# Normalised rows scattered into expert order: a routing pass whose pair table and row gathers give way to one read per slot

## What is computed

```
x = x + relu(adj_norm @ h @ W_neigh.T + b_neigh + h @ W_self.T + b_self)     # h = layernorm(x), adj is 2048 x 2048
z = layernorm(x)
top 2 of 8 experts for each row by softmax(z @ Wg + bg), weights normalised to sum to 1
x = x + sum over the two experts e of weight_e * (relu(z @ W1[e] + b1[e]) @ W2[e] + b2[e])   # 256 -> 1024 -> 256
```

## Time and profile before

| what | us |
|---|---|
| median of 3 runs (lowest, highest) | 459.83 (457.51, 461.18) |
| span of the profiled execution | 457.5 |
| time of the profiled execution | 457.51 |
| TensorE busy | 386.6 |
| VectorE, ScalarE, GpSimd busy | 331.8, 260.0, 198.4 |

### The profile page before, as it was taken

How to read it: one execution, slowest core, us unless ns; L and a number is a source line. 1 busy time by engine, 2 the same in 40 slices (tenths; PEclk the granted TensorE clock), 3 DMA queues, 4 the chain that set the end, 5 groups by cost and what they waited for, 6 DMA issues and landing times.

```text
span 457.5 us, 10329 instructions
## 1 busy us (share of the span) xinstructions
PE 386.6 (84%) x3029; PEld 373.1 (82%) x3029; DVE 331.8 (73%) x762; ACT 260.0 (57%) x507; POOL 198.4 (43%) x213
## 2 busy tenths in 40 slices
PE   0699899979989920899699989999799998899990
PEld 0477899979989910899699979998799998899990
DVE  5677688867868655388568886887768888688880
ACT  1244533424243150498478874887878887488870
POOL 3000004434543464035445653664645664365663
PEclk9999999999999965699799998999999999899996
DMA  8900445785776111847656776467676677557671
GB/s 250 392 13 0 183 145 203 158 189 154 209 168 183 47 25 25 333 143 248 181 186 224 222 240 174 114 218 230 228 223 224 209 206 242 152 147 225 209 219 14
DMA packets 34526, 81.85 MB, mean 179 GB/s; under 512 B 14797, under 2 KB 28493, under 8 KB 29648
## 3 DMA queue, kind: packets, MB, share of 16 engines
q1 hardware_dynamic: 25616, 73.21, 47.9%
q0 software_dynamic: 8896, 8.48, 10.7%
HBM read 74.51 MB, written 9.77 MB: 184 GB/s over the span
## 4 chain that ended last, share of the span: by engine, by line
PE 68%; DMA 12%; issue 8%; DVE 5%; ACT 2%; SPq 1%; POOLq 1%; POOL 1%; DVEq 0%; ACTq 0%
PE bank L823 28%; PE bank L966 8%; PE bank L967 7%; PE bank L968 7%; PE bank L857 5%; PE bank L859 5%; PE bank L858 5%; DMA adj_raw<-adj_t 4%; PE bank L935 2%; DMA zg<-z_rows,slot_pair 2%; DMA slot_pair<-pairs 2%; DMA y_c<-ws_t 2%; DMA pairs<-pair,slot_i 1%; DVE split L756 1%; PE bank L876 1%
## 5 line engine op out<-in xcount | busy, mean ns | idle before, releaser
L823 PE MATMUL bank<-zt,split 128*128 128x256 f32 x960 | 119.2, 284 | 1.4 <-DVE zt L761 1.4
L823 PEld LDWEIGHTS bank<-zt,split 128*128 128x128 f32 x960 | 117.2, 191 | 1.8 <-DVE zt L761 1.8
L469 ACT ACTIVATE split<-w_raw 128x1024 fp32r<-128x1024 f32 x84 | 87.0, 1072 | 37.5 <-PE bank L968 21.1
L756 DVE TENSOR_TENSOR split<-w_raw,split 128x1024 fp32r<-128x1024 f32 x84 | 100.6, 1220 | 6.5 <-ACT split L469 6.1
L384 POOL DMA_INDIRECT out<-y_c,kept x40 | 72.6, 1814 | 63.8 <-ACT y_c L513 55.8
L966 PE MATMUL bank<-split,h_hi 128*128 128x256 f32 x320 | 94.5, 295 | 0.0
L967 PE MATMUL bank<-split,h_hi 128*128 128x256 f32 x320 | 91.4, 286 | 0.0
L968 PE MATMUL bank<-split,h_lo 128*128 128x256 f32 x320 | 91.3, 285 | 0.0
L367 POOL DMA_INDIRECT zg<-z_rows,slot_pair x44 | 60.8, 1383 | 69.0 <-issue 45.3
L491 ACT ACTIVATE h_raw<-bank,b_sb 128x256 f32<-128x256 f32 x160 | 72.1, 482 | 18.6 <-PE bank L823 18.2
L782 DVE TENSOR_TENSOR h_lo<-h_raw,h_hi 128x512 fp32r<-128x512 f32 x80 | 55.3, 692 | 32.8 <-ACT h_hi L494 31.5
(11 more groups left out here) (122 smaller groups left out, 454.9 us busy)
## 6 DMA issues: line engine op xcount, KB each, us to landing
w_raw<-w SPq DMA_DIRECT2D x22, 2048.0 KB, 8.1
adj_raw<-adj_t SPq DMA_DIRECT2D x16, 1024.0 KB, 6.7
b_sb<-b SPq DMA_DIRECT2D x21, 128.0 KB, 5.1
x_sb<-x SPq DMA_DIRECT2D x4, 512.0 KB, 5.3
out<-x SPq DMA_DIRECT2D x16, 128.0 KB, 3.9
z_rows<-z SPq DMA_DIRECT2D x16, 128.0 KB, 3.9
zg<-z_rows,slot_pair POOLq DMA_INDIRECT x44, 3.5
out<-y_c,kept POOLq DMA_INDIRECT x40, 5.4
```

The costliest lines, as they stand in the source:

```text
L469: act.activation(w_split(b, 0)[:, cols], w_raw[:, b, cols], ACT.Copy).then_inc(w_hi_ready, 1)
L756: dve.tensor_tensor(w_split(b, 1)[:, cols], w_raw[:, b, cols], w_split(b, 0)[:, cols], ALU.subtract).then_inc(w_lo_ready, 1)
L823: last = pe.matmul(o, w, m, start=(n == 0), stop=(n == len(terms) - 1), skip_group_check=True)
```

## The change

The normalised row gets a tail of four words (its row number, the logit difference `DROP`, its first expert `FIRST`) in a ring of four buffers `zr`, and POOL's two indirect DMAs of a tile write the whole 1040-byte row into expert order in a DRAM tensor `rows`, where expert e owns CAP = 2304 rows. `z_rows`, `pairs`, its fill at the start and all `gather` calls are gone. After the last tile, SP writes 256 zero rows behind each expert's last row. A slot is one read of 256 rows. The row numbers for `out` are made by POOL from the tail and a table `past` that puts rows behind an expert's end out of bounds. The table is made on all 128 partitions.

```
 def store(i, b):
     sp.wait_ge(z_ready, i + 1)
     sp.dma_start(out[bass.ds(i * P, P), :], x1[:, b, :]).then_inc(x1_out[b], 16)
-    sp.dma_start(z_rows[bass.ds(i * P, P), :], z[:, b, :]).then_inc(z_out[b], 16)
...
+def load_rows(b, at):
+    sp.dma_start(zg[:, b, :, :], rows[bass.ds(at, SLOT), :].rearrange("(j p) w -> p j w", p=P)).then_inc(row_in[b], 16)
+def fill_after(e, done):
+    at = sp.value_load(fill_at[0:1, e:e + 1], min_val=0, max_val=E * CAP - SLOT)
+    sp.dma_start(rows[bass.ds(at, SLOT), :].rearrange("(j p) w -> p j w", p=P),
+                 zeros[:, None, :].to_broadcast([P, 2, RW])).then_inc(done, 16)
 def ahead(s, b):
     hold(w_lo_ready, 4 * s + 4)
-    if isinstance(s, int) and s == 0:
-        gathered(1)
     load_weights(b, expert(s + 2))
     hold(zt_ps, s + 1)
-    hold(idx_kept, s + 1)
-    hold(ex_ready, s + 1)
-    load_pairs(b, first_row(s + 2))
+    hold(kept_ready, s + 1)
+    hold(coef_step, 3 * s + 3)
+    load_rows(b, first_row(s + 2))
     if not isinstance(s, int) or s >= 1:
         hold(y_biased, s)
     e = expert(s + 1)
     ...  (b1_sb and b2_sb of slot s + 1, unchanged)
...
+sp.wait_ge(fill_ready, 1)
+fill_after(0, first_fill)
+for r in range(RING):
+    for c in range(TOPK):
+        sp.wait_ge(row_out[r][c], 16 * T // RING)
+sp.wait_ge(first_fill, 16)
+load_rows(0, 0)
+for e in range(1, E):
+    fill_after(e, fill_out)
 last = last_of(sp)
-gathered(0)
+sp.wait_ge(fill_out, 16 * (E - 1))
+load_rows(1, first_row(1))
 load_weights(1, expert(1))
```

GpSimd:

```
     for c in range(TOPK):
-        pool.indirect_dma_start(pairs, Rows(slot_i[:, b, c:c + 1], 0), pair[:, b, c, :],
-                                None).then_inc(pair_out[b][c], 16)
+        pool.indirect_dma_start(rows, Rows(slot_i[:, r, c:c + 1], 0), zr[:, r, :],
+                                None).then_inc(row_out[r][c], 16)
...
-def add(s, b):
-    for j in range(2):
-        pool.wait_ge(y_added[j], 16 * s)
-    settle(pool, "pool")
-    keep(1 - b)
-    pool.wait_ge(idx_kept, s + 1)
+def add(s, b, k):
+    pool.wait_ge(row_in[b], 16 * k + 16)
+    pool.tensor_tensor(kept[:, b, None, :], zg[:, b, None, :, TOKEN].bitcast(I32), past[:, bass.ds(s, 1), :],
+                       ALU.add).then_inc(kept_ready, 1)
+    for j in range(2):
+        pool.wait_ge(y_added[j], 16 * s)
+    pool.wait_ge(kept_ready, s + 1)
     pool.wait_ge(y_ready, 2 * s + 2)
     ...  (the two indirect DMAs with addition, unchanged)
 with pool.Fori(0, TURNS) as k:
     with pool.If(k < last + 1):
         for b in range(2):
-            gather(2 * k + b + 2, b, k + 1)
-            add(2 * k + b, b)
+            add(2 * k + b, b, k)
```

More of the change, by code:

```diff
@@ L43, in gnn_moe_kernel @@
     NS = 2 * TURNS + 2
[L44 to L48, removed]
+    RING = 4
+    RW = D + 4
+    TOKEN, DROP, FIRST = D, D + 1, D + 2
+    assert T % RING == 0 and T >= 3 * RING and DC == 2 and FC % 2 == 0 and WCH == F
+    CAP = N + SLOT
+    rows = nc.dram_tensor("rows", (E * CAP, RW), F32, kind="Internal").ap()
     with ExitStack() as ctx:
@@ L95, in gnn_moe_kernel @@
         warm = sb("warm", [P, 2])
[L96 to L110, removed]
+        slot_i = sb("slot_i", [P, RING, TOPK], I32)
+        thr = sb("thr", [P, 8])
+        tri = sb("tri", [P, E, E])
+        iota_s = sb("iota_s", [P, NS])
+        tb8 = sb("tb8", [P, 2, E, E])
+        cnt = sb("cnt", [P, 3, E])
+        ends = sb("ends", [P, 2, E])
+        ge = sb("ge", [P, 3, NS, E])
+        tab_f = sb("tab_f", [P, 6, NS])
+        past = sb("past", [P, NS, 2], I32)
+        zeros = sb("zeros", [P, RW])
+        fill_at = sb("fill_at", [1, E], I32)
+        past_f = sb("past_f", [P, NS, 2])
+        tab = sb("tab", [P, 2, NS], I32)
+        turn_slot = sb("turn_slot", [P, TURNS])
+        used = sb("used", [P, TURNS])
+        last_f = sb("last_f", [P, 1])
+        last_turn = sb("last_turn", [P, 1], I32)
         w_raw = sb("w_raw", [P, 2, WW])
@@ L298, in _ @@
                 hold(w_in[1], 16 * last + 32)
+                hold(row_in[1], 16 * last + 32)
                 for j in range(2):
-                    hold(z_got[1][j], 16 * last + 32)
                     sp.wait_ge(x1_out[j], 16 * T // 2)
@@ L386, in add @@
                                                 compute_op=ALU.add).then_inc(y_added[j], 16)
[L388 to L391, removed]
                 last = last_of(pool)
+                pool.wait_ge(past_ready, 1)
                 with pool.Fori(0, TURNS) as k:
@@ L655, in after, with placing @@
                             settle(dve, "dve")
+                    def placing(step):
+                        place(i - 3, (r + 1) % RING, k4 if r == 3 else k4 - 1, step)
                     dve.wait_ge(acc_done, i + 1)
@@ L659, in turn @@
                     if placed:
-                        place(i - 3, 1 - b, k + b - 2, 0)
+                        placing(0)
                     after(1)
@@ L668, in turn @@
                     if placed:
-                        place(i - 3, 1 - b, k + b - 2, 1)
+                        placing(1)
                     if choose:
@@ L718, in _ @@
                     for step in range(2):
-                        place(i, i % 2, i // 2, step)
+                        place(i, i % RING, i // RING, step)
                 tn = [0]
@@ L767, in slot @@
                         dve.wait_ge(y_ready, 2 * s - 2)
[L768 removed]
+                    dve.scalar_tensor_tensor(out=num[:], in0=zg[:, b, :, FIRST], scalar=tab_f[:, 0, bass.ds(s, 1)], in1=ex[:],
+                                             op0=ALU.is_equal, op1=ALU.max)
+                    dve.tensor_scalar(den[:], ex[:], 1.0, None, ALU.add).then_inc(coef_step, 1)
                     dve.wait_ge(coef_step, 3 * s + 1)
@@ L890, in ranks, with tile @@
                               skip_group_check=True).then_inc(rank_ps, 1)
-                def tile(i, b, back=3):
+                def tile(i, r, back=3):
+                    b = r % 2
                     pe.wait_ge(adj_lo, 2 * i + 1)
@@ L910, in _ @@
                 pe.wait_ge(g_done, T)
-                for i in range(4):
-                    tile(i, i % 2, back=i)
-                with pe.Fori(2, T // 2) as k:
-                    for b in range(2):
-                        tile(2 * k + b, b)
-                transpose_z(T - 2, 0)
+                for i in range(RING):
+                    tile(i, i, back=i)
+                with pe.Fori(1, T // RING) as k:
+                    for r in range(RING):
+                        tile(RING * k + r, r)
+                transpose_z(T - 2, RING - 2)
                 ranks(T - 3, 1)
                 logits(T - 2)
-                transpose_z(T - 1, 1)
+                transpose_z(T - 1, RING - 1)
                 logits(T - 1)
@@ L928, in transpose_slot @@
                 def transpose_slot(s, b, k):
-                    for j in range(2):
-                        pe.wait_ge(z_got[b][j], 16 * k + 16)
+                    pe.wait_ge(row_in[b], 16 * k + 16)
                     if not isinstance(s, int) or s >= 1:
```

167 lines of the change are left out of this document (77 added, 90 removed).

## The result

The changed kernel takes 472.8 us (471.1 to 476.3, 4 runs) against 460.5 of the kernel before: ratio 1.026, 95% interval 1.020 to 1.032. It is slower, as forecast (470). The profiled execution has a span of 469.5 and a time of 471.25; some 1.8 us lie around the span in this and every later profiled run, of both kernels (463.86 and 462.1 for the kernel before, run again). The 457.51 that I had taken for both time and span of the first profile may thus have been its span alone. Of the 2.8 us by which the median lies above the forecast, 1.8 are this.

The account below looks back on a forecast made before the run. TensorE was taken to pace both stages before the change, and a circle of waits of 13.5 us per slot to pace the experts after it. 203.7 + 18 x 13.5 + 23.7 = 470.4 us, range 455 to 484.

Parts of the forecast that it names:

- circle of waits: Experts: each slot's bias wait leads to the next through POOL and SP; period 13.5 us, bounds 12.1 and 15.5.
- A to the first add: Experts: from ScalarE starting a slot's weight split behind its waits (A) to POOL's first add; 3.6 us.
- the two adds: Experts, POOL: issue of a slot's two adds; 4.0 us, or 3.6 if the second is as short.
- `kept`, from the adds' end to its own: Experts, POOL: the count SP needs, ending with VectorE's weight split; 1.0 us, 0.27 if not held up.
- landing and wake: Experts: second bias load lands near an empty queue's time, 2.1 us, then ScalarE wakes, 0.1 us.
- Between the stages: From last scatter to slot 1: rows come 4.1 us sooner, but seven fills on SP turn that into 3.9 lost.
- A(1): Moment ScalarE starts slot 1's weight split behind its waits; forecast at 203.7 us, against 199.79 before.
- the aggregation, taken as nothing: Aggregation: one store less per tile and a larger scatter counted as no change; last scatter issued at 173.37 as before.
- The short circle: Rival, experts: `kept` precedes VectorE's split or adds take 3.6; period 12.4 to 13.1, 457 us, chance 0.20.
- the circle doesn't bind: Rival, experts: biases land before TensorE finishes y, gathers' waits go; period 11.9, 441.6 or 437 us, chance 0.10.
- the scatter that holds up the aggregation: Rival, aggregation: VectorE waits 1 us for a ring place in 12 tiles; 12 us more, 482, chance 0.05.
- The longer circle: Rival, experts: late bias landings (3.7) or TensorE's clock falling; period 14.3 to 15.5, 485 to 506 us, chance 0.10.

Follow-up runs that it names:

- either of two places: Changed kernel with SP's two bias loads moved ahead of the hold: 438.9 us; or with GpSimd making `kept` ahead of the add's wait: 439.4 us.

## Why the prediction was right, and where it was not

**The mechanism is shown.** The forecast rested on a circle of waits that can be read from the code: bias wait, adds, `kept`, SP's hold, biases. Opened at either of two places it vanishes, with 34 us. The signs named in advance are there: the bias wait in nearly every slot, SP's row load about 1.1 us after `kept`, TensorE waiting in small pieces for the low hidden parts (0.4 us in the mean, though the longest is 1.8 and not under 1), no wait of the transposes. One sign that was named for being wrong is there too: bias loads that land later than 3 us, in nine of 18 periods.

**The period, 13.5 forecast, 13.82 measured.** By its terms, for slot 5 (252.29 to 265.62, 13.33), slot 7 (279.85 to 294.20, 14.35) and the mean of all 18:

| term | forecast | slot 5 | slot 7 | mean |
|---|---|---|---|---|
| A to the first add | 3.6 | 3.46 | 3.46 | 3.46 |
| the two adds | 4.0 | 3.39 | 3.92 | 3.61 |
| `kept`, from the adds' end to its own | 1.0 | 0.34 | 1.29 | 0.65 |
| to the row load | 0.97 | 1.18 | 1.05 | 1.10 |
| to the second bias load | 1.72 | 1.73 | 1.74 | 1.77 |
| landing and wake | 2.2 | 3.23 | 2.89 | 3.24 |

The term that came out too small is the landing: 2.1 forecast, 3.0 in the median, from these rows of the second bias load:

```profile
DMA to landing us min/median/max: 2.8/3.0/10.8
```

I had taken it near the quickest 128 KB store (1.8). The Trainium skill's page "DMA: Bandwidth & Descriptors", section "Anatomy of one DMA — SWDGE (gpsimd) path", fits DMAs that GpSimd issues; applied to this load, which SP issues, the fit makes an estimate of 2.3, and the measurement is above that too.

The landing with its wake is 1.04 us too small in the mean, and three terms are too large: the adds by 0.39, `kept` by 0.35, the way to the first add by 0.14. That the sum is only 0.3 off is in part luck. `kept` has two forms. With a second add of 1.54 to 1.76 us it starts ahead of VectorE's split and is done in 0.9 or less; with one of 2.06 it falls into the split and ends with it. The second form, which the forecast took for every slot, comes in six of the 18 periods. The other thing that lengthens a period is a landing of 3.5 to 4.1 us, in four of them. Together they make the eight periods of 13.8 to 15.6: four with the late `kept` alone (14.35 to 14.59), two with the late landing alone (13.82, 14.23), two with both (15.49, 15.59). The other ten are 13.0 to 13.4. What makes those four landings late was not tried. The Trainium skill's rule that VectorE in its two-port mode locks GpSimd out (same page, section "SWDGE vs HWDGE vs iDMA") agrees with the end of `kept` at 288.52 and of the split at 288.50; whether the split runs in that mode no row shows.

**Between the stages** the steps held to a few tenths: first row load to the weights of slot 1 12.8 us (12.4 forecast), those to A(1) 15.1 (15.0), A(19) to the end 23.75 (23.76). The fills cost what was said.

**Where it failed: the aggregation, taken as nothing.** "In the aggregation SP loses one store per tile and the scatter grows ... about 4 us cover": I asked only whether the larger scatter could hurt, and didn't ask what the 16-byte one had cost. That the last scatter comes "as before, since POOL issues back to back there" failed with it: it stands 14.4 to 14.5 us behind the last aggregation matmul in both kernels, and that matmul moved from 159.0 to 151.8. The last scatter came at 166.32 and not at 173.37, 7.05 us sooner, and A(1) at 197.02 and not 203.7. The median on the page stood there to be read: 5.8 us for one scatter, 2 KB, to land. The Trainium skill's page "DMA: Bandwidth & Descriptors", section "Specifications", says that below 512 bytes the DMA engines read, modify and write. The run with 512-byte records agrees in that its scatters land sooner; that reading and writing is the reason, or 512 bytes the bound, no run here shows.

So the total is better than its parts, by luck: 6.7 us too late at A(1), and 18 times 0.32, 5.8 us, too little in the circle; 470.4 forecast against a span of 469.5. With only A(1) right the forecast would have been 464, with only the period right 476, both above the 457.51 of the kernel before.

**The rivals.** The short circle came in part: `kept` slipped in ahead of the split in 12 of 18 periods, and the adds took 3.4 us in ten of them, as that rival asked; the longer landing ate what they saved, and the shortest periods are 13.0. That the circle doesn't bind is refuted by 17 waits in the experts, the scatter that holds up the aggregation by TensorE's 103.56 busy of 103.67. The longer circle was real in part too: its price is seen in seven of 18 periods (14.2 to 15.6), by late bias landings as it said in three of them, and by `kept` beside VectorE's split in six. The clock had no part in it: the granted clock over the experts is 0.98 in both kernels.

## What to carry to other kernels

When a wait or a count moves behind other work on its engine, follow what is queued behind it on every queue until the chain either ends or comes back to its start: one that comes back sets a period if its sum is above the pace of the busiest engine, and its terms can be summed from the trace before the change is built. Order an in-order queue by when each transfer is needed, not by which buffer comes free: here two bias loads behind one hold turned a gain of some 21 us into a loss of 12. And where an edit removes a transfer, price what it was costing its neighbours, not only itself.

## What the hardware showed that I had not expected

- Writes of 16 bytes: an indirect DMA of 128 of them (two per tile) lands in 5.8 us in the median, one of 128 times 1040 bytes in 2.8, beside the same 1 MB loads. The small ones delay these loads (6.6 us to land in place of 5.1 with 512-byte records) and lengthen the aggregation from 103 or 104 us to 110 to 113.
- Waits of TensorE of 1.8, 2.9 and 3.4 us in the middle of dense work were each followed by a granted clock of 0.83 over 10 us (two profiles of the kernel before); one of 1.6 there, and those of up to 1.1 without the `z` store, left it at 1.00.
- 128 partitions that read one and the same 1 KB of DRAM (the second bias load, 128 KB in all) land in 3.0 us behind a row load of 266 KB and in 3.1 without it, while the 266 KB of different rows land in 2.8.
- An indirect DMA took 5.28 us to issue in place of 0.96 beside four back-to-back VectorE operations of 4.61 us on two float32 inputs; so it was in three profiles of the kernel before and its variants (5.0 to 5.6). In two of the changed kernel's variants it started as close behind them and took 1.8 and 1.9. What makes the difference was not tried.
